# Routing's front and first choice inside the second feed-forward stage, with that stage's normalised x written by ACT

## What is computed

```python
x = L0_attn_x
x = x + 0.5 * _L0_ffn_ref(_layernorm(x), ...)   # dense product plus 8 gated LoRA experts
x = x + _L0_attn_ref(_layernorm(x), ...)        # causal attention, 16 heads, relative bias
x = x + 0.5 * _L0_ffn_ref(_layernorm(x), ...)   # same weights again
x = x + 0.5 * _L1_ffn_ref(_layernorm(x), ...)   # routed: 4 of 16 experts, plus a shared one
x = x + _L1_attn_ref(_layernorm(x), ...)        # retention
x = x + 0.5 * _L1_ffn_ref(_layernorm(x), ...)   # routed again
```

```python
logits = x_flat.astype(jnp.float32) @ router_w.T
scores = jax.nn.sigmoid(logits)
s = scores + bias[None, :]
sg = s.reshape(-1, NG, EPG)
group_score = jax.lax.top_k(sg, 2)[0].sum(-1)
gidx = jax.lax.top_k(group_score, TKG)[1]
...
topk_idx = jax.lax.top_k(masked, K)[1]
tw = jnp.take_along_axis(scores, topk_idx, axis=1)
tw = tw / (tw.sum(-1, keepdims=True) + 1e-20)
```

## Time and profile before

| | us |
|---|---|
| median of 3 executions | 1351.33 (1351.0 to 1353.26) |
| the profiled execution's own time | 1355.15 |
| its span, first to last instruction | 1353.4 |
| PE busy / weight loads | 1261.7 (93%) / 1074.6 (79%) |
| DVE, ACT, POOL busy | 964.7 (71%), 765.2 (57%), 765.6 (57%) |
| mean granted PE clock | 0.964 of full |

### The profile page before, as it was taken

The page is one execution under the profiler, slowest core; times in us unless marked ns, Lnnn a source line. Parts: engine busy times, 40 slices in busy tenths (PEclk is TensorE's granted clock), DMA queues, the critical chain, the costliest instruction groups (busy, mean ns, idle before and its releaser), DMA issues. The chain is left out here.

```text
span 1353.4 us, 34803 instructions
## 1 busy us (share of the span) xinstructions
PE 1261.7 (93%) x10236; PEld 1074.6 (79%) x10236; DVE 964.7 (71%) x4100; ACT 765.2 (57%) x1805; POOL 765.6 (57%) x1010
## 2 busy tenths in 40 slices
PE   7899999998867799999779999999999979999998
PEld 5667777776746688888669999998988867888887
DVE  6678888887759455656458787888888847555554
ACT  2288888885364244444246667776677654444443
POOL 2288888885333645555335556575687554345543
PEclk9899999998878899999979999999999989999999
DMA  5199980000030112121112212121221112112121
GB/s 149 36 274 272 270 258 0 0 2 2 1 117 32 58 29 30 30 29 28 22 46 54 52 50 51 44 55 44 57 60 49 31 38 81 35 28 32 30 30 15
DMA packets 102887, 85.27 MB, mean 63 GB/s; under 512 B 10791, under 2 KB 90505, under 8 KB 102490
## 3 DMA queue, kind: packets, MB, share of 16 engines
q1 hardware_dynamic: 84084, 65.51, 17.6%
q0 software_dynamic: 17280, 16.17, 6.8%
q10 hardware_dynamic: 1382, 1.83, 0.5%
HBM read 20.92 MB, written 45.78 MB: 49 GB/s over the span
## 5 line engine op out<-in xcount | busy, mean ns | idle before, releaser
L1973 POOL TENSOR_TENSOR attn_z<-attn_top,attn_z 128x256 f32<-128x256 f32 x256 | 154.1, 612 | 35.3 <-DVE attn_top L1923 34.6
L1923 DVE CUSTOM_DVE_ANT_0 attn_z<-banks,rel_bias 128x128 f32<-128x128 f32 (+1 forms) x512 | 147.3, 353 | 23.4 <-PE banks L2056 18.0
L2492 POOL TENSOR_TENSOR ret_rotated<-ret_twins 128x512 f32<-128x512 f32 x64 | 82.1, 1283 | 132.8 <-DVE ret_twins L2402 132.7
L997 DVE SCALAR_TENSOR_TENSOR moe_block_act<-banks,moe_block_weights,moe_block_gated 128x128 f32<-128x128 f32 x276 | 77.7, 344 | 65.5 <-ACT moe_block_gated L1052 40.3
L2006 ACT ACTIVATE attn_prob<-banks 128x384 f32<-128x384 f32 x256 | 111.7, 488 | 20.8 <-PE banks L2066 14.4
L1542 DVE SCALAR_TENSOR_TENSOR moe_block_act<-banks,moe_block_weights,moe_block_gated 128x128 f32<-128x128 f32 x276 | 77.7, 344 | 63.0 <-ACT moe_block_gated L1636 39.6
L2555 ACT ACTIVATE ret_normed<-banks,ret_head_shift,ret_head_rstd 128x128 f32<-128x128 f32 x256 | 96.3, 458 | 45.5 <-DVE ret_head_shift L2426 45.2
L2066 PE MATMUL banks<-ident,attn_z 128*128 128x128 f32 x768 | 111.2, 280 | 0.7
L2066 PEld LDWEIGHTS banks<-ident,attn_z 128*128 128x128 f32 x768 | 82.2, 140 | 20.8 <-issue 14.2
L2587 PE MATMUL banks<-ret_x_hi,ret_hi 128*128 128x256 f32 x256 | 85.1, 332 | 1.9 <-ACT ret_gate L2548 1.0
L1026 POOL DMA_INDIRECT y_rows<-moe_block_y,moe_taken x37 | 58.7, 1585 | 46.6 <-ACT moe_block_y L1062 38.5
(11 more groups left out here) (359 smaller groups left out, 4060.0 us busy)
## 6 DMA issues: line engine op xcount, KB each, us to landing
slots<-moe_pad SPq DMA_DIRECT2D x12, 2560.0 KB, 23.4
ret_twins<-ret_twins SPq DMA_DIRECT2D x256, 64.0 KB
moe_stage<-in_moe_w SPq DMA_DIRECT2D x4, 576.0 KB, 6.8
bias_reversed<-scratch SPq DMA_DIRECT2D x1, 2048.0 KB, 9.5
y_rows<-moe_pad SPq DMA_DIRECT2D x1, 2048.0 KB, 9.3
back_of_seq<-y_rows SPq DMA_DIRECT2D x16, 128.0 KB, 2.3
out<-x_res SPq DMA_DIRECT2D x8, 256.0 KB, 2.5
ret_stage<-in_ret_w SPq DMA_DIRECT2D x16, 96.0 KB, 2.1
```

Of the source, the lines that this page charges most:

```text
L997: last = dve.scalar_tensor_tensor(act_f[:, i, at], ps_u[:, i, at], weights[:, s % 2, part, e:e + 1], gated[:, i, at], ALU.mult, ALU.mult)
L1923: last = dve.tensor_tensor_reduce(out=z[:, s, cols], in0=ps_s[:, i, cols], in1=bias, scale=1.0, scalar=-3.0e38, op0=ALU.add, op1=ALU.max, ...
L1973: pool.tensor_tensor(z[:, s, P:WIDTH], top[:, s, 1:2].to_broadcast([P, WIDTH - P]), z[:, s, P:WIDTH], ALU.subtract).then_inc(shifted1, 1)
L2492: pool.tensor_tensor(rotated[:, k % 2], twins[:, k % 2, 0], twins[:, k % 2, 1], ALU.add).then_inc(rotated_ready, 1)
```

## The change

1. In the second feed-forward stage (`scaled=True`) DVE no longer writes the normalised x. It writes `shift` = -mean * rstd (one 128x4 operation), and ACT writes x * rstd + shift, four instructions of 128x128, at the head of its step.
2. The routing's front becomes `RouteHead`, a pipeline of 11 steps (`HEAD_STEPS`) inside the second feed-forward stage's steps 0 to 10: statistics of group n as soon as `residual` of group n is done, shift and normalised rows one step later, transposes, x_hi and x_lo two steps later, the router three steps later. It has one bank for the transposes instead of two. The router now holds x stationary: 12 products of 16 columns per group, written straight in the layout that the choice wants, so the copy of 16x512 and the transposes back are gone.
3. The first choice (`Choice`, segment 0) runs on DVE in steps 7 to 10, six operations a step, followed by `classes`. `moe_route` begins with the ranking of segment 0; the second choice is spread over the first tiles as before, and its ranking comes after 11 tiles.
4. The weight split moves from the second feed-forward stage's steps 3 to 6 to its steps -1 to 2.
5. SP's loads for retention move from `moe_route`'s block to that of `moe_blocks`; the 16 parts' split there is one slot later. The clearing of semaphores (`retire`) moves from before `moe_route` to before `moe_blocks`.
6. Buffers of the routing share memory with attention's (`Arena`); POOL writes the token numbers after attention is done.

The core of the diff:

```diff
-            return [(1, in_last_iteration(engine, GROUPS // U, split[2], split[which]))] if split else []
+            return [(1, in_first_iteration(engine, GROUPS // U, split[2], split[which]))] if split else []
...
+            def shift_of(it, u):
+                p = u % 2
+                dve.wait_ge(rstd_done, count(it, u))
+                dve.scalar_tensor_tensor(shift[:, p, :], mv[:, p, :, 0], -1.0, rstd[:, p, :], ALU.mult, ALU.mult).then_inc(shift_done, 1)
...
+            return Steps(dve, GROUPS // U, U, [(3, shift_of if scaled else normalise), (2, router_shift), (4, layernorm), (2, gates), (0, residual)])
...
+            def normalise(it, u):
+                p = u % 2
+                xg = x_group(it, u)
+                act.wait_ge(shift_done, count(it, u))
+                wait_free(act, xn_transposed, count(it, u, 2))
+                for j in range(GROUP):
+                    last = act.activation(xn[:, p, j, :], xg[:, j, :], ACT.Identity, bias=shift[:, p, j:j + 1], scale=rstd[:, p, j:j + 1])
+                last.then_inc(xn_ready, 1)
...
+class RouteHead:
...
+            return Steps(dve, GROUPS, 1, [(-1, shift_of), (0, layernorm), (-2, split_x)])
...
+            return Steps(pool, GROUPS, 1, [(0, set_tokens), (0, inverse_std)])
...
+            return Steps(act, GROUPS, 1, [(-2, copy_x_hi), (-1, normalise), (-3, copy_logits)])
...
+                for j in range(GROUP):
+                    hi, lo = (part[:, g, j * P:(j + 1) * P] for part in (x_hi, x_lo))
+                    out = ps_logit[:, j * MOE_E:(j + 1) * MOE_E]
+                    pe.matmul(out, hi, r_hi, start=True, stop=False)
+                    pe.matmul(out, hi, r_lo, start=False, stop=False)
+                    last = pe.matmul(out, lo, r_hi, start=False, stop=True)
+                last.then_inc(routed, 1)
+
+            return Steps(pe, GROUPS, 1, [(-2, transpose_x), (-3, router)])
...
+            route = head.vector(dve)
+            for n in range(HEAD_STEPS):
+                ffn2.at(n, 0, 3)
+                route.at(n, 0, 1)
+                ffn2.at(n, 3)
+                route.at(n, 1)
+                if n == CHOICE_FIRST:
+                    choice.set_pads(dve)
+                if n >= CHOICE_FIRST:
+                    choice.topk(dve, 0, (n - CHOICE_FIRST) * 6, (n - CHOICE_FIRST) * 6 + 6)
+            choice.classes(dve, 0)
...
+            for n in range(-2, HEAD_STEPS):
+                ffn2.at(n, 0, 1)
+                route.at(n)
+                ffn2.at(n, 1)
...
+            for n in range(HEAD_STEPS):
+                ffn2.at(n, 0, 1)
+                route.at(n, 0, 1)
+                ffn2.at(n, 1, 3)
+                route.at(n, 1)
+                ffn2.at(n, 3)
...
             rank_tokens(0)
-            shared(9, 19)
+            shared(0, 11)
             rank_tokens(1)
-            shared(19, TILES)
+            shared(11, TILES)
```

More of the change, by code:

```diff
@@ L490, in moe_route @@
+def moe_route(nc, tag, banks, used, x_res, ident, w, slots, places, route, choice):
     I32 = mybir.dt.int32
@@ L809, in shared @@
                         copy_actT(t - 2)
[L811 to L822 removed]
+            choice.sigmoid(act, 1)
+            shared(0, TILES)
             copy_actT(TILES - 2)
@@ L2116, with front_phase @@
 LATE_FLIPS = {-5: (4, 5), -4: (6, 7)}
-LOOPS = 6
-def front_phase(nc, banks, used, x_res, first, attention, second, opening, background):
+LOOPS, HEAD_STEPS = 6, GROUPS + 3
+CHOICE_FIRST = SEG // GROUP + 3
+def front_phase(nc, first, attention, second, head, choice, opening, background):
     with ExitStack() as ctx:
@@ L2187, in _ @@
             ffn2.at(-1, 2)
-            for n in range(GROUPS):
-                ffn2.at(n)
+            route = head.tensor(pe)
+            for n in range(HEAD_STEPS):
[4 more added lines that the diff above has]
+                ffn2.at(n, 3)
         @block.scalar
@@ L2199, in _ @@
             quads.at(61)
-            for n in range(-1, GROUPS):
+            route = head.scalar(act)
+            for n in range(-1, HEAD_STEPS):
+                if n == CHOICE_FIRST:
+                    act.wait_ge(head.logits_ready, SEG // GROUP)
+                    choice.sigmoid(act, 0)
                 ffn2.at(n)
+                route.at(n)
 def bucket_one_hot():
```

523 lines of the change are left out of this document (260 added, 263 removed).

## The result

The changed kernel takes 1355.87 us (median of 20 executions) against 1351.51 us for the kernel before (median of 20, 1346.5 to 1356.0). Two of the changed kernel's 20 executions took 1457.55 and 2068.48 us, at a mean granted clock of 0.82 and 0.56; the others lie between 1348.38 and 1357.99, with a median of 1355.1, and the ratios here are made without them. The ratio is 1.0025, with a 95% interval of 1.0014 to 1.0035. A second series gave 1355.15 against 1351.18 us, ratio 1.0033 (1.0017 to 1.0049). I had forecast 1346.8 us and a gain of 4.5 us; the change costs some 3.4 to 4.5.

The account below looks back on a forecast made before the run. No engine full in the routing's front, DVE setting the feed-forward step (4.60 us); the first gather moves from 467.13 to 462.4, 4.7 us, rounded to 4.5, giving 1346.8 from 1351.33, range 1337 to 1357.

Parts of the forecast that it names:

- the term for the clock: Second feed-forward stage: one spell at 1.2 GHz fills PE's waits, leaving PE at 370.0 us after step 3.
- part 2: Feed-forward steps 0 to 6 with the routing's head: full step 5.9 us, 6.8 us of stalls, last product at 384.4.
- part 3: First choice on DVE after the last product: 18.3 us with nothing covering it, front's end at 402.7.
- change of block: From the front's last work to the start of the next block: 1.2 us.
- part 4: `moe_route` up to the last residual: 56.5 us instead of 61.7, end 460.4, first gather 461.6.
- rival (b): Feed-forward steps: waits put PE at 1.2 GHz through step 6, full step about 11 us; about 1356 us; chance 0.15.
- Rival (d): A tie: front's saving spent in slower steps and DVE's choice, 3 us above the sum; about 1350.5 us; chance 0.22.
- signs of being wrong: Residual 7 before 378 or after 392, clock 0.50 from 355 to 390, or first gather's landing over 5 us.
- Part 1: End of attention: ACT's normalising delays it by 2.3 us, first residual at 342.1 instead of 339.77.
- The stalls: DVE held by POOL's weight split in steps 0 to 3: 1.4, 1.9, 2.0 and 1.5, together 6.8 us.
- Part 5: SP's sixteen retention loads meet the first gathers: 0.8 us, bounded by 0 and 7.5.
- Rival (c): The loads make the first gather land up to 7.5 us late; about 1353.5 us; chance 0.07.

Follow-up runs that it names:

- Before_scaled: The kernel before with only ACT's normalising of the second feed-forward stage added: 1387.40 us on the second chip, ratio 0.9972 to the kernel before.
- norm_shared: split_in_route with the second stage's first three groups normalised on DVE, the other five on ACT: 1342.45 us, ratio 0.9927 to the kernel before.
- split_in_route: Changed kernel with three of four weight-split parts moved into the shared expert's last tiles: 1347.37 us, ratio 0.9978 to the kernel before.
- before_zero_low: The kernel before with POOL's four weight-split subtractions replaced by a fill with zeros: 1383.96 us on the second chip, ratio 0.9954 to the kernel before.
- split_dve_norm: split_in_route with the second stage's normalising back on DVE: 1386.96 us on the second chip, ratio 0.9966 to the kernel before.
- Choice_inside: Changed kernel with only the first choice put back among the shared expert's tiles: 1355.07 us, ratio 1.0030 to the kernel before.
- both_mixed: norm_shared with the first choice put back among the shared expert's tiles: 1350.12 us, ratio 0.9978 to the kernel before.
- Dve_norm: Changed kernel with only the second feed-forward stage's normalising put back on DVE: 1351.27 us, ratio 1.0010 to the kernel before.
- pool_in_route: split_in_route with ACT's casts kept in feed-forward steps 0 to 3, only POOL's subtractions moved: 1391.48 us on the second chip, ratio 1.0010 to the kernel before.

## Why the prediction was wrong

**The step that failed.** It is the term for the clock in part 2: "I take one such spell, which fills the waits and leaves PE at 370.0 after step 3. Then steps 4, 5, 6 on PE: 5.85, 4.25, 4.25". (These are PE's steps; the products of one step belong to the residual of the next.) The forecast let PE come back to 2.4 GHz once the waits were over. In the trace PE stayed at 1.2 GHz from 352 to 373. The products that the forecast has done at 370.0 end at 373.9, the next step of PE takes 7.2 us instead of 5.85, and only the last two have the forecast size (4.2 and 4.0). So residual 7 came at 389.38 instead of 384.4. That alone is 5.0 us, more than the whole gain. The second trace has its cold stretches elsewhere and residual 7 at 390.91.

**The sum.** Where to add up was right for the first part of the loss: 1.1 to 2.6 us of it are made before the first gather. That gather was forecast for 461.6 (462.4 with the loads) and came at 468.21. The 6.6 us are 5.0 of part 2, 0.4 of part 3, -0.8 for the change of block (forecast 1.2 us, here 408.1 to 408.5), 1.1 of part 4 and 0.9 between the last residual and the gather.

**The rivals.** What happened is rival (b), to which I gave 0.15. Its mechanism was right: a full step of PE at 1.2 GHz takes 10.3 us (363.4 to 373.7; it said about 11). Its length lies between my one spell and its "through step 6". The point against it did not hold: the head's products did fill PE from 373 to 384, and the clock was 0.77 all the same. That its price of about 1356 meets the median is in part luck, for by the first gather the traces show 1.1 to 2.6 us of loss where (b) has some 5. Rival (d) has a slip: 3 us more than the sum is 1349.8, not 1350.5. None of the signs of being wrong appeared (residual 7 lies between 378 and 392); the bounds were too wide to catch an error of 5 us, when the whole gain was 4.7.

**Part 1.** I said 342.1 for residual 0, and 344.0 with a split's stall: it came at 343.98. Before_scaled measures ACT's normalising alone there at +3.3 us (3.1 on its own chip) instead of 2.3; norm_shared gets 2.8 of it back. PE's first product with the third group's x came at 334.83, forecast 334.1.

**The stalls.** Forecast 1.9, 2.0 and 1.5 us in steps 1 to 3, measured 2.20, 2.19 and 1.63 (the durations less 0.16); in step 0, forecast 1.4, `shifted` took 1.97 us instead of its usual 0.19. The Trainium skill, page "SBUF — State Buffer", section "SBUF: two separate sides", says that the first to take the shared pair of ports holds it for the whole instruction; by that rule the stall ends with POOL's subtraction, and the trace agrees to 0.02 us. So the stalls were sized well, and what I did not see is what comes behind them. They are 6.0 us on DVE, but taking the splits out gives 10.5 us in this stage, and 4.6 of these in steps 4 to 7, where there is no split any more and the changed kernel has PE at 1.2 GHz for much of the time. That the stalls and casts together bring these cold stretches is shown by split_in_route, and by before_zero_low for the kernel before; through which wait of PE the clock falls, and when, is argued and not shown, for the two traces of the changed kernel differ in it and split_dve_norm has a short cold stretch without them.

**Part 3.** The first choice: 18.3 us forecast from the last product to the front's end, and from residual 7 (389.38) to the end of `classes` (408.1) it is 18.7. Right. I called this uncovered time a cost. Choice_inside and both_mixed show that it hardly is one: under cover DVE reaches the last residual 0.4 to 2.2 us earlier, and POOL's later scatters take that away again.

**Part 4.** Forecast 56.5 us from the route's start to the last residual; from 408.5 to 466.1 it is 57.6. The excess is of the size of DVE's first wait, 1.39 us at 409.49, for the ranking on a PE at 1.2 GHz; that it comes from there is not shown. The first gather goes out 2.1 us after the last residual, forecast 1.2.

**Part 5.** Forecast 0.8 us for the loads, measured 0.4: the first product of the routed experts comes 2.98 us after the first gather, it was 2.60. Rival (c) is out.

SyncE's queue and PE, changed kernel:

```profile
467.52 7.45 SPq L2963 DMA_DIRECT2D ret_stage<-in_ret_w  x16
```

```profile
471.19 0.48 PE L1118 MATMUL banks<-ident,moe_taken 128*128 128x128 f32 x1 [5.81 <-DMA moe_taken<-slots,small]
```

**What stays open.** Up to the first gather the traces account for 1.1 to 2.6 us of the 3.4 to 4.5 us by which the medians differ. The rest lies behind the first gather, where the part that follows took 882.9 us in both traces of the changed kernel and 886.3 and 884.0 in those of the kernel before, while the medians want it the other way round. Dve_norm is a like case: its gather is 2.7 us ahead of the kernel before, and the medians are equal. Which executions have a cold stretch late in the program, and whether the change has a hand in it, two traces of each can't tell. For the same reason the sum made on one execution of before (1355.15 us, 3.8 above its median) could be trusted up to the gather and not to the end. The 3.0 us for the casts come from kernels on two different chips, and no kernel has the subtractions beside the head without the casts.

## What to carry to other kernels

Before work is taken from the engine that sets the step, look whether that engine's time is work or a stall: here the kernel before lost 7.4 us to a weight split on POOL, the change moved the split under new victims, and moving three of its four parts to where DVE reads PSUM was worth 7.8 us, more than the head and the choice in the front (3 to 4 us up to the gather). PE's clock can fall after such waits and stay low for steps in which nothing waits any more (here 4.6 us on top of 6.0), so price a stall with the steps after it, and give the clock its own range. And a serial piece that was moved out of its cover was here neither lost nor won by that alone; ask which third engine comes free by it (here POOL, 13 us) and give that time a use.

## What the runs showed of the chip that was not expected

An operation on 128x4 elements (0.16 us by itself) took 2.36 us beside a subtraction on POOL: its small size gave it no protection, while a product with one input in PSUM, 128x256, was not held at all. DVE's normalising, 1.10 us, also took 1.73 us beside a plain fill on POOL that reads nothing.

On the second chip the kernel before takes 41 us longer. In the shared expert PE and ACT stand still together there for several microseconds (ACT for 5.39 us before 416.90), with no releaser that the profile can name; PE's timeline of pool_in_route:

```profile
420.27 0.66 PE L925 MATMUL banks<-ident,moe_gated 128*128 128x128 f32 x2 [6.72 <-issue]
```

No run here shows where these pauses come from.
